# Splitting expert weights two blocks per instruction in a graph layer with an 8-expert feed-forward

## The reference, cut to what matters

```python
# t: (384, 1024) after a layer norm
logits = t @ switch_w + switch_b
route_prob = softmax(logits); routes = argmax(route_prob)
for e in range(8):
    h = gelu(t @ w1[e] + b1[e])      # w1[e]: 1024 x 512
    y = h @ w2[e] + b2[e]            # w2[e]: 512 x 1024
    out = where(routes == e, y, out)
out = out * max(route_prob)
x = x + out
```

## Time and profile before

| what | value |
|---|---|
| median of 3 runs | 667.09 us (663.29, 667.09, 669.68) |
| the profiled execution's own time | 665.32 us |
| span of the profiled execution | 663.6 us |
| mean granted TensorE clock | 0.961 of full speed |
| DVE busy in the span | 457.2 us (69%) |
| ACT busy in the span | 317.2 us (48%) |
| PE busy in the span | 581.2 us (88%) |

### The profile page before, as it was taken

One profiled execution on the slowest core, in us unless ns is written; L12 is line 12 of the kernel. 1 busy time (PEld: TensorE's weight loads), 2 busy tenths in 40 slices (PEclk: granted clock), 3 DMA queues, 4 the chain that ended last, 5 costly groups with the idle time before them and its releaser, 6 DMA issues.

```text
span 663.6 us, 9424 instructions
## 1 busy us (share of the span) xinstructions
PE 581.2 (88%) x3143; PEld 530.8 (80%) x3143; DVE 457.2 (69%) x751; ACT 317.2 (48%) x467; POOL 218.7 (33%) x184
## 2 busy tenths in 40 slices
PE   3899889999999999999998889999799569888860
PEld 2888788888999999998887889999688557676650
DVE  6799997525444554644797878677747947999962
ACT  3455444310333333432745645665435614999950
POOL 5665442555553990600089450000012100000001
PEclk9899999999999999999999999999999759999985
DMA  8476765400346334563222432221254303899925
GB/s 296 137 210 202 185 179 191 133 26 1 103 127 225 121 127 158 161 205 96 63 96 67 137 112 95 63 93 65 96 169 154 111 17 127 313 413 411 411 86 206
DMA packets 32961, 102.68 MB, mean 155 GB/s; under 512 B 5376, under 2 KB 9536, under 8 KB 32928
## 3 DMA queue, kind: packets, MB, share of 16 engines
q1 hardware_dynamic: 27792, 90.02, 40.1%
q0 software_dynamic: 4992, 11.72, 5.7%
q10 hardware_dynamic: 144, 0.52, 0.3%
HBM read 96.65 MB, written 5.60 MB: 154 GB/s over the span
## 4 chain that ended last, share of the span: by engine, by line
PE 57%; DVE 17%; DMA 10%; issue 6%; POOL 4%; ACT 3%; SPq 1%; POOLq 0%; DVEq 0%; ACTq 0%
PE ps L1421 31%; PE ps L1435 8%; DVE wsp L894 5%; DMA rowbuf<-in_dst_rows 5%; DVE big L894 3%; PE ps L1554 3%; DMA raw_x<-in_w_experts 3%; PE ps L1544 2%; PE ps L1649 2%; PE ps L1529 2%; PE ps L1491 2%; PE ps L1472 2%; POOL work L476 2%; PE ps L1564 1%; POOL row_buf L474 1%
## 5 line engine op out<-in xcount | busy, mean ns | idle before, releaser
L1421 PE MATMUL ps<-big,wsp 128*128 128x384 f32 x1680 | 306.4, 340 | 15.9 <-DVE wsp L894 10.9
L1421 PEld LDWEIGHTS ps<-big,wsp 128*128 128x128 f32 x1680 | 294.4, 190 | 24.2 <-DVE wsp L894 9.1
L894 DVE TENSOR_TENSOR wsp<-raw,wsp 128x1024 fp32r<-128x1024 f32 x121 | 164.9, 1377 | 32.2 <-ACT wsp L595 29.8
L595 ACT ACTIVATE wsp<-raw 128x1024 fp32r<-128x1024 f32 x89 | 93.5, 1053 | 41.1 <-PE ps L1435 19.5
L1435 PE MATMUL ps<-wsp,big 128*128 128x512 f32 x288 | 66.7, 391 | 4.0 <-DVE snm L1100 3.5
L494 POOL DMA_INDIRECT edge_table<-ef,eidx x48 | 51.2, 1066 | 50.9 <-DMA edge_table<-ef,eidx 32.4
L1435 PEld LDWEIGHTS ps<-wsp,big 128*128 128x128 f32 x288 | 53.7, 188 | 15.6 <-DVE snm L1100 3.8
L602 ACT ACTIVATE big<-ps,bias 128x384 f32 x24 | 14.0, 583 | 82.5 <-PE ps L1421 82.5
L905 DVE SCALAR_TENSOR_TENSOR big<-ps,bias,big 128x384 f32 x24 | 14.8, 618 | 51.0 <-ACT big L602 50.9
L564 POOL DMA_DIRECT2D slot_y<-maskb x8 | 4.5, 563 | 117.6 <-DVE maskb L1338 117.6
L894 DVE TENSOR_TENSOR big<-raw_x,big 128x1024 fp32r<-128x1024 f32 x32 | 37.8, 1216 | 4.8 <-ACT big L772 4.7
(11 more groups left out here) (230 smaller groups left out, 844.1 us busy)
## 6 DMA issues: line engine op xcount, KB each, us to landing
raw<-in_w_stream SPq DMA_DIRECT2D x89, 512.0 KB
raw_x<-in_w_experts SPq DMA_DIRECT2D x32, 512.0 KB, 6.7
raw<-in_w_experts SPq DMA_DIRECT2D x32, 512.0 KB
rowbuf<-in_src_rows SPq DMA_DIRECT2D x16, 192.0 KB, 4.1
rowbuf<-in_dst_rows SPq DMA_DIRECT2D x16, 192.0 KB, 5.0
rowbuf<-in_rowb POOLq DMA_DIRECT2D x6, 512.0 KB, 6.1
slot_y<-maskb POOLq DMA_DIRECT2D x8, 256.0 KB, 5.5
tok<-in_x SPq DMA_DIRECT2D x3, 512.0 KB, 4.0
```

Of the source, the lines that this page charges most:

```text
L595: nc.scalar.activation(wsp[:, 0, slot, :], raw[:, slot, :], ACT.Copy).then_inc(w_hi, 1)
L894: return nc.vector.tensor_tensor(dst, value, hi.bitcast(F32), ALU.subtract)
L1421: ins = nc.tensor.matmul(ps[:, bank, 0:N], wsp[:, a, slot, k * P:(k + 1) * P], moving[:, b, k, :], start=(k == 0 and n == 0), stop=(k == K ...
```

## The change

ACT and DVE each get a function `prep_two`, which splits two neighbouring slots by one instruction over 128 x 2048 elements. ACT waits for both landings, and for a `w_started` one higher than for the first block alone; its instruction adds 2 to `w_hi`. DVE waits for a `w_hi` of two blocks and adds 2 to `w_lo` at the end of its instruction. For slots 6 and 7, whose split halves lie in different tensors, `prep_two` calls `prep_x` twice. The loads stay one per block. In ACT's order copy_up now follows after two splits, not three. The 8 splits ahead of the stage, and those in the branch for overflowing experts, stay single.

```diff
+        def raw_two(k):
+            return raw[:, k:k + 2, :] if k < RING else raw_x[:, k - RING:k - RING + 2, :]
+        def split_two(k, part):
+            if k < RING:
+                return wsp[:, part, k:k + 2, :]
+            return bigs[3][:, part, 0:2 * D].rearrange("p (k n) -> p k n", k=2)
...
+            def prep_two():                                    # ACT
+                slot = (q_no.n - Q_MOE + RING) % XRING
+                if slot == XRING - 2:
+                    prep_x()
+                    prep_x()
+                    return
+                for k in range(2):
+                    act.wait_ge(raw_in[slot + k], used[slot + k].add(16))
+                act.wait_ge(w_started, q_no.value + 1 - (XRING - 2))
+                nc.scalar.activation(split_two(slot, 0), raw_two(slot), ACT.Copy).then_inc(w_hi, 2)
+                q_no.add(2)
...
             copy_up(0)
-            prep_x()
-            prep_x()
+            prep_two()
             hidden(0)
-            prep_x()
-            prep_x()
+            prep_two()
             for e in range(EXPERTS - 1):
                 if e < EXPERTS - 2:
-                    for _ in range(3):
-                        prep_x()
+                    prep_two()
                 copy_up(e + 1)
                 if e < EXPERTS - 2:
-                    prep_x()
-                prep_x()
-                prep_x()
+                    prep_two()
+                prep_two()
                 low_rows_of_y(e)
                 hidden(e + 1)
-                prep_x()
-                prep_x()
+                prep_two()
             low_rows_of_y(EXPERTS - 1)
...
+            def prep_two():                                    # DVE
+                slot = (q_no.n - Q_MOE + RING) % XRING
+                if slot == XRING - 2:
+                    prep_x()
+                    prep_x()
+                    return
+                dve.wait_ge(w_hi, q_no.add(2))
+                lo(split_two(slot, 1), raw_two(slot), split_two(slot, 0)).then_inc(w_lo, 2)
...
             routes()
-            prep_x()
-            prep_x()
+            prep_two()
             hidden(0)
-            prep_x()
-            prep_x()
+            prep_two()
             for e in range(EXPERTS - 1):
                 if e < EXPERTS - 2:
-                    for _ in range(4):
-                        prep_x()
-                prep_x()
-                prep_x()
+                    prep_two()
+                    prep_two()
+                prep_two()
                 rows_of_y(e)
                 hidden(e + 1)
-                prep_x()
-                prep_x()
+                prep_two()
             rows_of_y(EXPERTS - 1)
```

## The result

The changed kernel takes 675.23 us (median of 20 runs, 669.36 to 678.78) against 666.51 us (20 runs, 663.29 to 669.68): a ratio of 1.0129, 95% interval 1.0104 to 1.0153. It is slower by about 8.6 us. The forecast was 670.8, with a range to 674.5: the sign was right, the size was less than half.

A forecast was written before the change was run, and what follows sets the result against it. The prediction took the transfers (10.83 us a period at 412 GB/s) as the bound, DVE just inside. Its terms, 1.1 + 1.9 + 0.7 = +3.7 us on the 667.09 us median, gave 670.8 us, range 665.5 to 674.5.

The forecast's parts named there:

- What bounds the kernel: Expert stage, per period: transfers at 412 GB/s set 10.83 us, with DVE just inside at 10.54 us.
- The price of a pair: One 128x2048 split: 2.29 us on DVE, 1.89 us on ACT; 0.06 us saved per pair on DVE.
- Term 1: Start of the expert stage: first loads into slots 4 and 5 go out later, stream ends 1.1 us later (0.3 to 1.9).
- Term 2: Lag from slot 5's landing to y grows, paid once at the stage's end: +1.9 us (1.0 to 3.0).
- Term 3: Later releases leave 3.8 blocks in flight instead of 5.4: 0.12 us for each of six periods, +0.7 us.
- The upper end of term 3: Slot 1 keeps a 6.0 us landing, making periods 11.55 us: 0.72 us more in each of six, 4.3 us.
- the queue starves: Rival: upper end of Term 3 plus Term 1 and Term 2, 674.4 us; periods over 11.3 us, under 395 GB/s; chance 0.15.
- The gain: Rival: DVE's saving shortens seven periods by 0.18 us each, 665.8 us, or 664.1 with cheaper pairs; chance 0.08.

## Why the prediction was wrong

**What bounds the kernel** was read rightly in the main: the transfers, at 411 to 412 GB/s in all five periods, with DVE just inside them. The margin was thinner than I wrote. 10.83 us is the last period alone; the three before it took 10.74 to 10.75 us, and in the second DVE was busy for all of its 10.74. DVE's saving, 0.1 us of busy time per period, bought nothing.

**The price of a pair** was right: 2.28 to 2.29 us on DVE and 1.91 to 1.92 on ACT, against 2.29 and 1.89.

**Term 1** (+1.1) held in direction. The first load went out 5.0 us after copy_up(0) began (566.54 after 561.57), where it was 3.0, so 2.0 us later against 1.9 forecast, and the first y came 0.6 us later. One input was wrong: I let a lone load land after 3.3 us and its neighbour 1.27 us later. In the changed kernel the first two loads were issued 0.6 us apart on idle transfer engines (DMA share 0.00 from 564 to 566). They landed after 4.7 and 5.4 us, where the first two of before, 1.1 us apart, had taken 3.3 and 4.1. The four loads of the group (line 394 of the changed kernel, issues from 560 to 570 us):

```profile
DMA to landing us min/median/max: 4.7/5.3/5.4
```

That fits two loads which share the engines, so that both land late; it is one pair of loads in one execution.

**Term 2** (+1.9) was right in size where it shows: in the last period ACT begins the pair (4,5) as it lands, at 631.11, and y follows at 635.34, 4.2 us, where it was 2.25. It reached the end of the stage too: counted from copy_up(0), the sixth y is 5.5 us later and the eighth 5.6. But the pair's longer way acts twice. As a lag it is paid once; as part of the 5.24 us of the loop it makes each load late, in every period, and that second effect belongs to term 3.

**Term 3** is the step that failed, in the sentence "Nearest is the first, so most of the rate stays". I had the depth right (3.8 blocks in flight forecast; the median landing of 5.9 us and eight blocks per 11.7 us give an estimate of 4.0) and the mechanism by name. But I priced it at 0.12 us per period, as if the rate stayed, and the rate fell to 376 GB/s.

What the term measured can't be read off the 4.8 us by which the five periods grew, since the forecast itself put terms 1 and 2 into them (with its own part about 3.5 us in all, an estimate: 0.1 us at the first y, 3.6 at the sixth). In its own terms it is the landings that count. The last load of slot 5 ahead of the sixth y landed 66.0 us after copy_up(0) began, and 69.4 us in the changed kernel, 3.4 us later, where terms 1 and 3 together allowed 1.7 by then. With term 1 at its 1.1, term 3 comes to 2.3 us in place of 0.6 (an estimate). The profiled execution is a quick one. In that of the pairs with an earlier start, at 675.08 us close to the changed kernel's median, the five periods take 2.8 us more, and term 3 would be some 5 us.

The argument failed in two places. It took the rate that went with landings of 5.3 to 6.0 us in one row for what such landings give. With one split of delay they went with 411 GB/s, but landings of 4.9 to 5.5 us with two splits of delay went with 388, and those of the changed kernel with 376. And it let the landing time give way as far as the shorter queue asked, down to 4.2 us for slot 0. It gave way only in part: slot 5's landings went from 8.3 to between 5.3 and 7.5 us, too long for the 5.24 us behind them.

The upper end of term 3 kept a landing of 6.0 us, put the tight slot at 1 instead of 5, and came to 4.3 us for six periods. With that end the sum was 674.4, and the median is 675.2. The rival "the queue starves" is thus the case that came, a little beyond its price, and its own signs were met: stage under 395 GB/s, periods over 11.3 us (11.60 in the fourth). That its price came so near is partly luck, with the wrong slot and a landing shorter than most. I gave it 0.15 because I weighed one row (358 GB/s with three blocks in flight) against another (412 with landings of 5.3 to 6.0 us) and took the side of the second.

**Slips that didn't decide.** The slices near 410 GB/s are 36 to 38; slice 35 has 313. In term 3, 10.83 less 4.2 and 6.5 us leaves 6.6 and 4.3, not 6.2 and 4.2. The gain's lower end leaves out 0.18 us per period: with 0.6 us less in each of seven it would be 662.9, not 664.1.

**Not explained by the stage**: the two medians differ by 8.7 us, the two profiles by 7.2, and 1.6 of these lie outside the changed part. I have no cause for the 1.6. The other 1.5 are likely in the periods, since the profile of pairs that lies near the median has longer ones (61.19 us), but this isn't shown for the changed kernel itself.

**The gain** was the rival that leaned on the Trainium skill. "Perfetto Trace Analysis" there, section Optimizing Scalar/DVE Operations, says that grouping into larger operations can improve throughput if the engine is saturated. DVE had no idle time in the first two of the five periods before (10.54 of 10.54 and 10.74 of 10.74 us), and its busy time did fall, to 10.43 us, yet the kernel became slower. The section's other sentence is that breaking up instructions may allow work to be completed sooner where Scalar or Vector aren't saturated but cause bubbles on other engines. The trace of the changed kernel, which went the other way, agrees with it: DVE sat idle for 1.95 and 2.31 us ahead of the pair (4,5) in the first two periods, and PE waited 3.18 us before a down where it had waited 1.37.

## What to carry to other kernels

In a ring of buffers, write down the loop for each slot: landing, each reader in turn, release, issue, landing. Merging two blocks into one instruction nearly doubles each reader's part of that loop (2.3 to 4.2 us here) to save some 0.06 us of overhead on DVE; that pays only where the loop has several us to spare at the landing times that the trace shows under load, not at those of an idle queue. Where transfers set the pace, look for idle transfer time at the start of the stage: moving four splits ahead of a wait gave 1.6 us here (0.25%, hardly outside the noise).

## What the runs showed of the hardware

The transfer rate depends on how the loads are issued, though the DMA share stays near 1 (0.97 to 1.03 in these three): 412 GB/s with over five 512 KB loads in flight (an estimate from the landings), 388 with each load two splits late, 355 when these also came in twos. Loads of 256 KB over 64 partitions ran at 252 GB/s with a DMA share of 1.03 (the stretch from 590 to 640 us of the kernel before, so cut):

```profile
590.00:640.00 50.00, 35.09 (x128) 27.34 (x129) 31.59 (x29) 30.14 (x35) 1.65 (x3) 0.83 1.03 252
```

Loads of the same size over all 128 partitions, in rows of 2 KB, ran at 391 GB/s. And the granted TensorE clock, 1.00 in all full periods before, has a mean of 0.87 and 0.85 in the second and fourth period of the changed kernel. In the second, PE resumed at 590.88 after a wait of 3.18 us before down. The clock was 1.00 until 592, then 0.60 and 0.55 in the next two stretches of 2 us, near 1.2 GHz (0.5 of full speed), and 1.00 again from 596 (PE in order of time, the two halves of that down):

```profile
590.88 2.52 PE L1718 MATMUL ps<-big 128*128 128x512 f32 x8 [3.18 <-DVE big L913]
...
593.62 3.02 PE L1718 MATMUL ps<-big 128*128 128x512 f32 x8
```

Before, the same eight took 2.12 and 1.98 us. The chain of waits of these periods runs through the loads, so no part of the loss is put down to the clock.
